# Third FFN layer in (row, feature) form, with the h2 rows stationary, and TensorE's slot order turned

## The chip, the cores and the metric

The kernel runs on one core of a Trainium2 chip. The time is the device time of one execution in microseconds; the time before is 2948.12 us, the median of 3 runs (2947.69 to 2948.82). The profile is one further execution, of 2946.45 us.

## The reference, cut to what matters

The input is x (16 batches, 1024 nodes, 256 features). A graph attention block comes first, then a mixture of 8 experts (E = 8), each a three-layer FFN applied to every row. All experts run on all rows; a gate w, one vector of 8 weights for each of the 1024 nodes, sums them:

```
x = x + attention(layernorm(x), adj)                       # per batch 1024 x 1024
x = x + ffn(layernorm(x))
ffn:  w = softmax(mean over batch of x @ Wr + br)          # 1024 x 8
      h = relu(bn(x @ W1[e] + b1[e]))                      # per expert e
      h = relu(bn(h @ W2[e] + b2[e]))
      y = h @ Wo[e] + bo[e]
      out = sum over e of y * w[:, e]
```

All products are made from split operands: an fp32 value is a "hi" part in fp32r and a "lo" rest in fp32r, and one product is the three matmuls hi*hi, hi*lo and lo*hi.

## The kernel before, in words

`attention_block` (lines 145 to 792) fills roughly the first quarter of the time, `ffn_block` (lines 795 to 1195) the rest. The change is in `ffn_block` alone.

A tile is 512 rows (CT = 4 groups of 128) of one batch; a batch has CH = 2 tiles, and there are 16 batches, so 32 tiles. A step is one expert on one tile: 8 steps a tile, US = 16 steps a batch, 256 in all. Each engine runs `slot(b, u, last)` for u = 0 to 15 in a hardware loop over b of 15 iterations (B - 1), and then the 16 slots once more, written out. Slot u works ahead by different distances: layer 1 of step u + 3, layer 2 of step u + 2, layer 3 of step u + 1. So the pipeline of a step runs over several slots:

- TensorE, `layer` (L944): 12 matmuls for a layer, each 128 x 128 stationary (a block of weights, hi or lo) by 128 x 512 moving (the activations in (feature, row) form, 512 rows). It writes z1_ps, z2_ps or y_ps, two PSUM banks each. `split_matmul` (L50) issues the three matmuls of a product at L52, L53 and L54.
- ScalarE: `bn_relu` (L1048) of layer 1, the hi part of h1 (L1065), `bn_relu` of layer 2.
- VectorE: the lo part of h1 (L1127), the product of h2 with the gate (L1140), the hi part of h2 (L1144), the lo part of h2 (L1146).

Layer 3 sums all eight experts of a tile into y_ps, in (feature, row) form, since the gate is already in h2. At the end of a tile (u % 8 == 7) ScalarE copies y_ps to yT_sb (L1055), TensorE turns it with 8 transposes into turn_ps (`transpose_y`, L935 to 942), and VectorE adds the residual rows from x1_sb (L1153, `out_ready`). SyncE then stores the tile and loads the next one into the same buffer (L869 to 875). `transpose_x` (L925) turns the normalised rows of the next tile in slot u % 8 == 4, into the same PSUM tile turn_ps.

The order on TensorE in a slot is: layer 1 of u + 3, transposes if any, layer 2 of u + 2, layer 3 of u + 1. The order is written out by hand and each engine keeps it. Where a layer starts, TensorE waits for the lo part of its input; for the first expert of a tile layer 3 waits also for `yT_ready`, since y_ps is opened anew.

The gate table, transposed, lay in yT_sb at the start (`wT_sb`), before the first tile used it.

Of the kernel before, what the change touches and what calls it, by code (L numbers as in the profile page):

```python
# [23 lines left out]
ALU = mybir.AluOpType  # L24
# [3 lines left out]
P = 128  # L28
# [766 lines left out]
def ffn_block(nc, B, Wo, x1_dram, w_dram, out, ident, minus_half, node_table, w12_hi, w12_lo,  # L795
# [11 lines left out]
    with ctx:  # L807
        def sb(name, shape, dt=FP32):
            return ctx.enter_context(nc.sbuf_tensor(name, shape, dt))
# [4 lines left out]
        def sem(name):  # L814
# [15 lines left out]
        yT_sb = sb("yT_sb", [P, KB, BANK])  # L830

        wT_sb = yT_sb[0:E, :, :].rearrange("e c n -> e (c n)")
# [12 lines left out]
            step_done yT_ready out_psum out_ready  # L845
# [19 lines left out]
        def _(sp):  # L865
# [17 lines left out]
            sp.dma_start(w_dram.rearrange("e c n -> e (c n)"), wT_sb).then_inc(w_stored, DMA)  # L883
# [40 lines left out]
        def _(pe):  # L924
            def transpose_x(n):  # L925

                pe.wait_ge(norm.xn_ready, n)
                wait(pe, S["out_ready"], n - 2)
# [5 lines left out]

            def transpose_y(n):  # L935

                pe.wait_ge(S["yT_ready"], n)
                for s in range(CT):
                    for d in range(KB):
                        at = (s % 2) * D + d * P  # L940
                        last = pe.transpose(turn_ps[:, s // 2, at:at + P], yT_sb[:, d, s * P:(s + 1) * P], ident[:, :])  # L941
                last.then_inc(S["out_psum"], 1)

            def layer(acc, w_hi, w_lo, x_hi, x_lo, first, last):  # L944

                for m in range(KB):
                    for k in range(KB):
                        at = slice(k * D + m * P, k * D + (m + 1) * P)
                        done = split_matmul(pe, acc[:, m, :], w_hi[:, at], w_lo[:, at], x_hi[:, k, :], x_lo[:, k, :],
                                            first and k == 0, last and k == KB - 1)  # L950
                return done
# [17 lines left out]
            def slot(b, u, last):  # L969
                ok, c, e, n = step_at(b, u, 3, last)  # L970
# [13 lines left out]
                if u >= 0 and u % E == E - 1:  # L984
                    transpose_y(b * CH + (u // E + 1))
# [6 lines left out]
                ok, c, e, n = step_at(b, u, 1, last)  # L992
                if ok:
                    pe.wait_ge(S["h2_lo_ready"], n)
                    if u == -1:
                        pe.wait_ge(S["table_ready"], 1)
                        pe.wait_ge(S["wo_lo_ready"], 2)
                        pe.wait_ge(S["wo_lo_pool_ready"], 2)
                    if e == 0:
                        wait(pe, S["yT_ready"], b * CH + (u + 1) // E)  # L1000
                    layer(y_ps, wo_hi[:, e, :], wo_lo[:, e, :], h2_hi[n_par(u + 1)], h2_lo[n_par(u + 1)],
                          e == 0, e == E - 1).then_inc(S["step_done"], 1)
# [16 lines left out]
            for u in range(1 - LOOK, 0):  # L1019
                slot(0, u, B == 1)  # L1020
# [202 lines left out]
```

## Time and profile before

| what | value |
|---|---|
| median of 3 runs | 2948.12 us (2947.69 to 2948.82) |
| the profiled execution | 2946.45 us, span 2944.7 us |
| TensorE busy | 2884.2 us, 98% of the span |
| VectorE busy | 1931.2 us, 66% |
| ScalarE busy | 1697.9 us, 58% |
| GpSimd busy | 730.2 us, 25% |
| one loop iteration of the FFN part | 16 steps, 15 iterations and one written out |

The span is the time from the first instruction to the last; the execution's own time has 1.75 us more around it. Starts of matmuls, rather than their durations, tell what TensorE costs: the matmuls are pipelined, one is some 0.39 us long and the next starts after some 0.23 us.

### The profile page before, as it was taken

The numbers are of one execution on the slowest core, as the hardware profiler recorded it, in microseconds if no ns is written. First come the engines' busy times: TensorE is split into PE (matmuls) and PEld (weight loads), VectorE is DVE, ScalarE is ACT, GpSimd is POOL, SyncE is SP. The second block draws the span as 40 slices with busy tenths as digits, with TensorE's granted clock in tenths as the row PEclk, the third lists the DMA queues.
The fourth block names the chain that finished last, engine by engine and source line by source line (L and its number), as shares of the span: only waits on it lengthen the run. The fifth ranks groups of instructions, "written<-read, shape, count | busy, mean of one in ns | idle before, by whom it ended". The sixth has DMA issues, their size and how long they took to land.

```text
span 2944.7 us, 42543 instructions
## 1 busy us (share of the span) xinstructions
PE 2884.2 (98%) x14806; PEld 2423.9 (82%) x14806; DVE 1931.2 (66%) x2843; ACT 1697.9 (58%) x2620; POOL 730.2 (25%) x894
## 2 busy tenths in 40 slices
PE   7999999998999999999999999999999999999998
PEld 7989898998888888888888888888888888888887
DVE  7999999996555555655556565556555565655554
ACT  7889888987444545444444445454544444454544
POOL 5888888887100000000000000000000000000000
PEclk9999999999999999999999999999999999999999
DMA  4444444443100000000000000000000000000000
GB/s 153 150 155 155 150 156 152 156 141 111 57 15 14 21 21 14 14 14 14 14 14 14 14 14 14 14 14 14 23 20 14 14 14 14 14 14 14 14 15 15
DMA packets 86037, 145.60 MB, mean 49 GB/s; under 512 B 7744, under 2 KB 63464, under 8 KB 86000
## 3 DMA queue, kind: packets, MB, share of 16 engines
q1 hardware_dynamic: 86000, 145.13, 14.7%
q8 instruction: 20, 0.33, 0.0%
q14 instruction: 17, 0.14, 0.0%
HBM read 111.52 MB, written 33.59 MB: 49 GB/s over the span
## 4 chain that ended last, share of the span: by engine, by line
PE 75%; DVE 0%; ACT 0%; issue 0%
PE z_ps L54 16%; PE z_ps L52 16%; PE z_ps L53 16%; PE y_ps L54 8%; PE y_ps L53 8%; PE y_ps L52 8%; PE turn_ps L931 1%; PE turn_ps L941 1%; PE y_ps L1016 0%; PE turn_ps L965 0%; PE y_ps L965 0%; PE z_ps L1009 0%; PE y_ps L1009 0%; ACT h L1048 0%; DVE h L1140 0%; DVE h_lo L1146 0%
## 5 line engine op out<-in xcount | busy, mean ns | idle before, releaser
L1048 ACT ACTIVATE h<-z_ps,bn_shift,bn_scale 128x512 f32<-128x512 f32 x1024 | 741.8, 775 | 1077.5 <-PE z_ps L54 1075.9
L1127 DVE TENSOR_TENSOR h_lo<-h,h_hi 128x1024 fp32r<-128x1024 f32 x256 | 321.6, 1256 | 762.5 <-ACT h_hi L1065 762.5
L86 POOL TENSOR_TENSOR ffn_vareps<-ffn_mv,ln_eps 128x4 f32<-128x4 f32 x32 | 6.4, 201 | 1880.0 <-DVE ffn_mv L80 1880.0
L52 PE MATMUL z_ps<-h_hi,w_hi 128*128 128x512 f32 x1024 | 410.3, 401 | 0.0
L54 PE MATMUL y_ps<-h_hi,wo_lo 128*128 128x512 f32 x1024 | 406.8, 397 | 0.0
L1140 DVE TENSOR_TENSOR h<-h,w_bc 128x1024 f32<-128x1024 f32 x256 | 313.8, 1226 | 140.9 <-ACT h L1048 137.0
L54 PE MATMUL z_ps<-h_hi,w_lo 128*128 128x512 f32 x1024 | 405.8, 396 | 0.0
L52 PE MATMUL z_ps<-xT_hi,w_hi 128*128 128x512 f32 x1024 | 405.2, 396 | 0.0
L53 PE MATMUL z_ps<-xT_lo,w_hi 128*128 128x512 f32 x1024 | 405.1, 396 | 0.0
L54 PE MATMUL z_ps<-xT_hi,w_lo 128*128 128x512 f32 x1024 | 405.0, 396 | 0.0
L53 PE MATMUL z_ps<-h_lo,w_hi 128*128 128x512 f32 x1024 | 405.0, 395 | 0.0
L53 PE MATMUL y_ps<-h_lo,wo_hi 128*128 128x512 f32 x1024 | 404.7, 395 | 0.0
L52 PE MATMUL y_ps<-h_hi,wo_hi 128*128 128x512 f32 x1024 | 402.3, 393 | 2.0 <-DVE h_lo L1146 2.0
L1146 DVE TENSOR_TENSOR h_lo<-h,h_hi 128x1024 fp32r<-128x1024 f32 x256 | 313.8, 1226 | 8.7
L52 PE MATMUL attn_ps<-wh_hi,pT_hi 128*128 128x256 f32 x1024 | 306.1, 299 | 0.0
L53 PE MATMUL attn_ps<-wh_lo,pT_hi 128*128 128x256 f32 x1024 | 289.2, 282 | 0.0
L54 PE MATMUL attn_ps<-wh_hi,pT_lo 128*128 128x256 f32 x1024 | 289.1, 282 | 0.0
L1065 ACT ACTIVATE h_hi<-h 128x1024 fp32r<-128x1024 f32 x256 | 271.3, 1060 | 9.3
L53 PEld LDWEIGHTS y_ps<-h_lo,wo_hi 128*128 128x128 f32 x1024 | 192.4, 188 | 49.0
L52 PEld LDWEIGHTS y_ps<-h_hi,wo_hi 128*128 128x128 f32 x1024 | 192.3, 188 | 48.5 <-DVE h_lo L1146 2.4
L52 PEld LDWEIGHTS z_ps<-xT_hi,w_hi 128*128 128x128 f32 x1024 | 192.6, 188 | 47.7
L54 PEld LDWEIGHTS z_ps<-xT_hi,w_lo 128*128 128x128 f32 x1024 | 192.5, 188 | 46.8
(128 smaller groups left out, 4876.6 us busy)
## 6 DMA issues: line engine op xcount, KB each, us to landing
adj_sb<-in_adj SPq DMA_DIRECT2D x128, 512.0 KB, 3.4
x_sb<-in_x SPq DMA_DIRECT2D x64, 256.0 KB, 2.8
x_scratch<-x_sb SPq DMA_DIRECT2D x128, 128.0 KB, 1.8
ffn_x<-x_scratch SPq DMA_DIRECT2D x32, 512.0 KB, 3.3
out<-ffn_x SPq DMA_DIRECT2D x32, 512.0 KB, 2.9
w_stage<-in_L_ffn_W SPq DMA_DIRECT2D x16, 256.0 KB, 4.0
w_bc<-w_scratch SPq DMA_DIRECT2D x8, 512.0 KB, 7.3
w_bc<-in_L_ffn_Wo SPq DMA_DIRECT2D x4, 512.0 KB, 5.9
```

The costliest lines, as they stand in the source:

```text
L52: pe.matmul(out, w_hi, x_hi, start=first, stop=False)
L53: pe.matmul(out, w_hi, x_lo, start=False, stop=False)
L54: return pe.matmul(out, w_lo, x_hi, start=False, stop=last)
L86: pool.tensor_tensor(self.vareps[:, :], self.mv[:, :, 1], self.ln_eps[:, :], ALU.add) \
L931: last = pe.transpose(turn_ps[:, d, s * P:(s + 1) * P], norm.xn[:, s, d * P:(d + 1) * P], ident[:, :])
L941: last = pe.transpose(turn_ps[:, s // 2, at:at + P], yT_sb[:, d, s * P:(s + 1) * P], ident[:, :])
L1048: return act.activation(dst[:, m, :], src[:, m, :], ACT.Relu, bias=bn_shift[layer][:, col], scale=bn_scale[layer][:, col])
L1065: act.activation(h1_hi[n_par(u + 3)][:, :, :], h1[:, :, :], ACT.Copy).then_inc(S["h1_hi_ready"], 1)
L1127: dve.tensor_tensor(h1_lo[i][:, :, :], h1[:, :, :], bits(h1_hi[i][:, :, :]), ALU.subtract) \
L1140: dve.tensor_tensor(h2[:, :, :], h2[:, :, :], w_bc[:, c, e, :].unsqueeze(1).to_broadcast([P, KB, BANK]), ALU.mult).then_inc(S["gated_ready ...
L1146: dve.tensor_tensor(h2_lo[i][:, :, :], h2[:, :, :], bits(h2_hi[i][:, :, :]), ALU.subtract) \
```

## The change

Layer 3 is computed with the operands swapped: the stationary operand is a 128 x 128 block of h2 (128 features by 128 rows), the moving one 256 columns of Wo, and the result is 128 rows by 256 features, the form in which the output is stored. One product of three matmuls is needed for each of 4 row groups and 2 halves of the contraction: 24 matmuls of 256 columns in place of 12 of 512. y_ps then holds rows, VectorE adds the residual straight from y_ps, and ScalarE's copy, the transposes and the tile yT_sb go. On TensorE layer 3 of step u now stands at the beginning of slot u; before, it was layer 3 of step u + 1 at the end of slot u. VectorE's addition moves from slot 7 of a tile, behind the work on h2 of slot 7, to slot 6, behind the work on h2 of that slot. Instead of `yT_ready`, TensorE waits for `out_ready` at the end of slot 7 of a tile. `transpose_x` waits for `xT_lo_ready` of the tile before in place of `out_ready`.

```diff
-        yT_sb = sb("yT_sb", [P, KB, BANK])
-        wT_sb = yT_sb[0:E, :, :].rearrange("e c n -> e (c n)")
+        wT_sb = sb("wT_sb", [E, TB * P])
...
             def transpose_x(n):
                 pe.wait_ge(norm.xn_ready, n)
-                wait(pe, S["out_ready"], n - 2)
+                wait(pe, S["xT_lo_ready"], n - 1)
...
-            def transpose_y(n):
-                pe.wait_ge(S["yT_ready"], n)
-                for s in range(CT):
-                    for d in range(KB):
-                        at = (s % 2) * D + d * P
-                        last = pe.transpose(turn_ps[:, s // 2, at:at + P], yT_sb[:, d, s * P:(s + 1) * P], ident[:, :])
-                last.then_inc(S["out_psum"], 1)
...
+            def layer_rows(e, x_hi, x_lo):
+                for s in range(CT):
+                    rows, acc = slice(s * P, (s + 1) * P), y_ps[:, s // 2, (s % 2) * D:(s % 2 + 1) * D]
+                    for k in range(KB):
+                        cols = slice(k * D, (k + 1) * D)
+                        opens = e == 0 and k == 0 and s % 2 == 0
+                        pe.matmul(acc, x_hi[:, k, rows], wo_hi[:, e, cols], start=opens, stop=False,
+                                  skip_group_check=True)
+                        pe.matmul(acc, x_hi[:, k, rows], wo_lo[:, e, cols], start=False, stop=False,
+                                  skip_group_check=True)
+                        done = pe.matmul(acc, x_lo[:, k, rows], wo_hi[:, e, cols], start=False,
+                                         stop=e == E - 1 and k == KB - 1, skip_group_check=True)
+                return done
...
             def slot(b, u, last):            # TensorE
+                if u >= 0:
+                    pe.wait_ge(S["h2_lo_ready"], b * US + (u + 1))
+                    layer_rows(u % E, h2_hi[n_par(u)], h2_lo[n_par(u)]).then_inc(S["step_done"], 1)
...
-                if u >= 0 and u % E == E - 1:
-                    transpose_y(b * CH + (u // E + 1))
...
-                ok, c, e, n = step_at(b, u, 1, last)
-                if ok:
-                    pe.wait_ge(S["h2_lo_ready"], n)
-                    if u == -1:
-                        pe.wait_ge(S["table_ready"], 1)
-                        pe.wait_ge(S["wo_lo_ready"], 2)
-                        pe.wait_ge(S["wo_lo_pool_ready"], 2)
-                    if e == 0:
-                        wait(pe, S["yT_ready"], b * CH + (u + 1) // E)
-                    layer(y_ps, wo_hi[:, e, :], wo_lo[:, e, :], h2_hi[n_par(u + 1)], h2_lo[n_par(u + 1)],
-                          e == 0, e == E - 1).then_inc(S["step_done"], 1)
+                if u >= 0 and u % E == E - 1 and not (last and u == US - 1):
+                    pe.wait_ge(S["out_ready"], b * CH + (u // E + 1))
...
                 slot(0, u, B == 1)
+            pe.wait_ge(S["table_ready"], 1)
+            pe.wait_ge(S["wo_lo_ready"], 2)
+            pe.wait_ge(S["wo_lo_pool_ready"], 2)
...
             def slot(b, u, last):            # ScalarE
-                if u >= 0 and u % E == E - 1:
-                    act.wait_ge(S["step_done"], b * US + (u + 1))
-                    act.activation(yT_sb[:, :, :], y_ps[:, :, :], ACT.Copy).then_inc(S["yT_ready"], 1)
...
-                if u >= 0 and u % E == E - 1:
+                if u >= 0 and u % E == E - 2:
                     t = u // E
-                    dve.wait_ge(S["out_psum"], b * CH + (t + 1))
+                    dve.wait_ge(S["step_done"], b * US + (u + 2))
                     dve.wait_ge(S["residual_ready"], b * CH + (t + 1))
                     rows = x1_sb[t][:, :, :].rearrange("p s d -> p (s d)")
-                    dve.tensor_tensor(rows, turn_ps[:, :, :].rearrange("p k c -> p (k c)"), rows, ALU.add) \
+                    dve.tensor_tensor(rows, y_ps[:, :, :].rearrange("p k c -> p (k c)"), rows, ALU.add) \
                         .then_inc(S["out_ready"], 1)
```

## Rows read from the trace of the kernel before

**Rows 1.** The page: busy times; VectorE's tenths and the granted clock in 40 slices.

```profile
PE 2884.2 (98%) x14806; PEld 2423.9 (82%) x14806; DVE 1931.2 (66%) x2843; ACT 1697.9 (58%) x2620; POOL 730.2 (25%) x894
...
DVE  7999999996555555655556565556555565655554
...
PEclk9999999999999999999999999999999999999999
```

**Rows 2.** Windows of 137.8 us, each an FFN iteration: busy (count), clock, DMA, GB/s.

```profile
744.70:882.50 137.80, 137.80 (x607) 111.38 (x606) 78.32 (x90) 67.13 (x84) 9.94 (x7) 1.00 0.05 16
1433.90:1571.70 137.80, 137.80 (x609) 111.43 (x608) 80.68 (x92) 67.16 (x85) 9.18 (x6) 1.00 0.04 15
```

**Rows 3.** Timeline of SyncE: the same store in two iterations that follow each other.

```profile
1441.12 0.38 SPq L871 DMA_DIRECT2D out<-ffn_x  x1
1578.96 0.39 SPq L871 DMA_DIRECT2D out<-ffn_x  x1
```

**Rows 4.** Timeline of TensorE around transpose_y and layer 3: start, length.

```profile
1499.88 0.40 PE L54 MATMUL z_ps<-xT_hi,w_lo 128*128 128x512 f32 x1
1500.11 1.04 PE L941 MATMUL turn_ps<-ident,yT_sb 128*128 128x128 f32 x8
1500.90 0.48 PE L52 MATMUL z_ps<-h_hi,w_hi 128*128 128x512 f32 x1
1501.22 0.39 PE L53 MATMUL z_ps<-h_lo,w_hi 128*128 128x512 f32 x1
...
1503.77 0.39 PE L52 MATMUL y_ps<-h_hi,wo_hi 128*128 128x512 f32 x1
...
1506.58 0.39 PE L52 MATMUL z_ps<-xT_hi,w_hi 128*128 128x512 f32 x1
```

**Rows 5.** Timeline of TensorE in the attention part, 256 columns, 24 in a row.

```profile
385.74 0.28 PE L53 MATMUL attn_ps<-wh_lo,pT_hi 128*128 128x256 f32 x1
385.86 0.28 PE L54 MATMUL attn_ps<-wh_hi,pT_lo 128*128 128x256 f32 x1
...
388.49 0.60 PE L462 MATMUL head_ps<-ident,x_sb 128*128 128x128 f32 x4
```

**Rows 6.** TensorE's waits over the whole span: us in total, times, longest.

```profile
PE y_ps L52 <- DVE h_lo L1146: 2.0, 1, 2.0
PE turn_ps L941 <- ACT yT_sb L1055: 1.1, 1, 1.1
```

**Rows 7.** Timeline of VectorE at a tile's end.

```profile
1429.33 1.23 DVE L1146 TENSOR_TENSOR h_lo<-h,h_hi 128x1024 fp32r<-128x1024 f32 x1
1433.97 1.23 DVE L1127 TENSOR_TENSOR h_lo<-h,h_hi 128x1024 fp32r<-128x1024 f32 x1 [3.41 <-ACT h_hi L1065]
1439.74 1.22 DVE L1153 TENSOR_TENSOR ffn_x<-turn_ps,ffn_x 128x1024 f32<-128x1024 f32 x1
```

**Rows 8.** Timelines of ScalarE and TensorE at the same place.

```profile
1428.59 1.03 ACT L1055 ACTIVATE yT_sb<-y_ps 128x1024 f32<-128x1024 f32 x1 [1.35 <-PE y_ps L54]
...
1434.85 0.39 PE L52 MATMUL y_ps<-h_hi,wo_hi 128*128 128x512 f32 x1
```

**Rows 9.** The chain of waits at the end of the span: start, us, what.

```profile
2937.56 0.25 PE y_ps L54
2937.81 0.02 issue
2937.83 1.03 ACT yT_sb L1055
2938.86 0.04 issue
2938.91 1.11 PE turn_ps L941 x8
2940.01 0.02 issue
2940.04 1.23 DVE ffn_x L1153
```

**Rows 10.** Groups by form: attention weight loads, then a matmul of 258 fp32 columns.

```profile
L53 PEld LDWEIGHTS attn_ps<-wh_lo,pT_hi 128*128 128x128 f32 x1024 | 195.7, 191 | 1.7
L476 PE MATMUL head_ps<-wx,hT 128*128 128x258 f32 x480 | 119.0, 390 | 0.0
```

**Rows 11.** DMA queues: window 744:883; window 883:2812; a small load's us to landing.

```profile
q8 instruction: 5, 0.08, 0.2%
...
q1 hardware_dynamic: 18816, 29.36, 4.5%
...
a_sb<-in_L_gnn_a SPq DMA_DIRECT2D x2, 1.0 KB, 2.4
```

More of the change, by code:

```diff
@@ L844, in ffn_block @@
             z1_ready h1_ready h1_hi_ready h1_lo_ready z2_ready relu2_ready gated_ready h2_hi_ready h2_lo_ready
-            step_done yT_ready out_psum out_ready
+            step_done out_ready
             featT_psum featT_ready logits_psum logits_ready top_ready centred_ready exp_ready total_ready
@@ L882, in _ @@
             sp.wait_ge(S["wT_ready"], 1)
-            sp.dma_start(w_dram.rearrange("e c n -> e (c n)"), wT_sb).then_inc(w_stored, DMA)
+            sp.dma_start(w_dram.rearrange("e c n -> e (c n)"), wT_sb[:, :]).then_inc(w_stored, DMA)
             sp.wait_ge(w_stored, DMA)
@@ L1035, in copy_gate @@
                 act.wait_ge(S["wT_psum"], 1)
-                act.activation(wT_sb, y_ps[0:E, :, :].rearrange("e k c -> e (k c)"), ACT.Copy) \
+                act.activation(wT_sb[:, :], y_ps[0:E, :, :].rearrange("e k c -> e (k c)"), ACT.Copy) \
                     .then_inc(S["wT_ready"], 1)
```

## The prediction

> **What bounds the kernel now.** The page comes first: TensorE is busy 98% of the span at full granted clock, while VectorE and ScalarE stand at 66% and 58% [rows 1]. Then the windows of one FFN iteration: TensorE is busy for all of the 137.80 us, in the first iteration and in a later one, with VectorE at 81 and ScalarE at 67 [rows 2]. Last the waits: in the whole FFN part TensorE waits once for h2 (2.0 us) and once for yT_sb (1.1 us), both at the very end [rows 6]. So the FFN part lasts as long as TensorE's queue takes from start to start, and an edit counts by what it does to that sum. Two stores of the same tile slot lie 1578.96 - 1441.12 = 137.84 us apart [rows 3]: that is the iteration.
>
> I price TensorE's pieces by starts. Eight transposes: without them the first matmul of layer 2 would start at 1500.11 and the second 0.233 later; the second starts at 1501.22, so the eight cost 1501.22 - 1500.11 - 0.233 = 0.87 us [rows 4]. An iteration has 48 layers and 4 such bundles (two of x, two of y): (137.84 - 4 x 0.87) / 48 = 2.799 us a layer, 0.2333 us a matmul of 512 columns; layer 3 in the timeline, 1503.77 to 1506.58, agrees [rows 3, 4].
>
> **The change, part by part.**
>
> 1. The transposes of y go: 31 times 0.87 us on the bounding engine, -27.0 us. The 32nd belongs to the end of the span, below.
>
> 2. Layer 3 becomes 24 matmuls of 256 columns. The columns streamed are the same, 6144; what is new is 12 more matmuls and 12 more weight loads a step. The FFN part has no such matmul, but the attention part has: 128 x 128 stationary, 256 moving columns, fp32r, the order hi, hi, lo, summed into half a bank. From 385.74 to the transpose behind the block at 388.49 are 23 starts: 2.75 / 23 = 0.1196 us; another pair gives 0.12 [rows 5]. That is 2.9 ns more than half of 0.2333. 24 x 0.1196 to 0.1200 is 2.87 to 2.88 us against 2.80, so +0.073 us a step (I take the longer baseline's value, 0.1197 rounded), and for 256 steps +18.7 us. Weight loads are no bound of their own at that pace: in those same attention rows each lasts 191 ns while they follow each other every 0.12 us [rows 5, 10]. Ends: below, the pace of the transposes, 8 in 0.87 us or 0.109 us a load and matmul (24 make 2.62 us, -46 us in all) [rows 4]; above, a matmul of 258 columns in plain fp32: each is 390 ns long against 0.28 us for the attention matmuls [rows 5, 10], and if the starts spread in that proportion, 0.167 us each, it would be 256 x (4.01 - 2.80) = +310 us. Its number format is another, so I give that end no weight; the value of the same form stands. The decisive point is thin: 1.7 ns a matmul more than 0.1197 eats the whole gain.
>
> 3. The turned order. Listed one behind the other, layers were 1(u+3), 2(u+2), 3(u+1), 1(u+4), ...; they are 3(u), 1(u+3), 2(u+2), 3(u+1), ...: the same sequence, with the loop's seam moved from before layer 1 to before layer 3. Distances between a layer and its consumer stay, apart from the 0.87 us that go and the 0.07 that come. Price nothing. Each iteration is busy throughout with the branch in it [rows 2], so the seam costs nothing today, with queued matmuls covering it.
>
> 4. The new wait. Layer 3 of a tile's first expert now needs `out_ready`. VectorE makes it in its slot 6: behind the lo part of h2 (start 1429.33, 1.23 long, ends 1430.56). The last layer 3 of the old tile was done at 1428.59, when ScalarE began its copy, so the addition (1.22 us, the same size and also out of PSUM) runs 1430.6 to 1431.8 [rows 7, 8]. TensorE's layer 3 stood at 1434.85 with the transposes in front; without them it stands at 1433.98 [rows 4, 8]. The slack is 2.1 us. Price nothing. Queued behind the wait on TensorE's queue are the branch (second tile of a batch) and layer 3 itself; VectorE's next instruction, L1127, came at 1433.97 and waited 3.41 us for ScalarE, so the earlier addition delays nothing there [rows 7]. It leaves VectorE's slot 7, where it stood alone at 1439.74.
>
> 5. ScalarE loses 32 copies of 1.03 us, SyncE's store and reload start some 9 us sooner, `transpose_x` has a wait long satisfied. All beside TensorE; nothing. The own wT_sb and the three waits before slot 0 are work of the prologue in the same order; nothing (ends: 1 us either way).
>
> 6. The end of the span. From the last layer 3 the chain went copy, transposes, addition: ScalarE began at 2937.83, VectorE at 2940.04 [rows 9]. Now VectorE follows at once: -2.2 us. The 0.07 us of the last layer is in the 18.7.
>
> Sum: -27.0 + 18.7 - 2.2 = -10.5 us. The profiled execution took 2946.45 us, so 2935.9; the median of the runs is 1.67 us above it, so 2937.6, written as 2938 (-0.3%).
>
> 7. More instructions. An iteration has 609 matmuls and 608 weight loads [rows 2] and would have 192 - 16 = 176 more of each: some 1,570 in place of 1,217. In the first iteration the instruction queue brought 5 packets, 0.08 MB, which is 16 KB a packet and some 66 bytes an instruction; in the next 14 iterations it brought none (the only queue with traffic from 883 to 2812 us is q1) [rows 11]. So a body of about 5 blocks stays on the chip; the new one, by the same bytes, is 6.3 blocks, and no row shows a body of that size. If it doesn't stay, the branch back needs a fetch. The first pass, whose blocks come while it runs, has no idle time [rows 2, 11], so blocks in sequence are hidden; only the target of the branch could be late. The ends for that are nothing (queued matmuls cover it) and 2.4 us, the landing time of a small load [rows 11], 14 times. I take nothing, being nearer to the row of a body that is held.
>
> The Trainium skill, Runtime: NRT & Kernel Launch, section Instruction fetch mechanics, says that a taken branch whose target is outside a window of two pages must wait for a fetch. The trace disagrees: a loop of 5 blocks ran 14 times with no instruction packet. The same section gives TensorE 128 KiB, eight blocks of 16 KiB, in contradiction to its two; by that figure (an estimate) the new body, 6.3 blocks laid over 7 or 8 block borders with one fetched ahead, lies right at the edge. By the one rule every pass pays today already, and the change brings nothing new; by the other the case turns on the body's place.
>
> **The rivals.**
>
> A. Refetch at the seam (slower). The longer body isn't held, and each of 14 branches exposes up to 2.4 us: up to 2937.6 + 34 = 2971. Moreover the branch now stands right behind the wait of part 4, so fewer matmuls are queued ahead of it. It decides from 10.5 / 14 = 0.75 us a branch. For it: nothing of that length was seen to be held; against: 5 blocks are held with ease and a first pass hides all its fetches. Half exposed, 2954. Chance 12%.
>
> B. Matmuls of 256 columns cost more beside h2 than in attention (same, or a little slower). There the stationary blocks were written long before; here VectorE and ScalarE write their pair tiles beside them. 2 to 3 ns more each: 2950 to 2956. For it: only the smallness of the margin; against: in the attention part, the first quarter of the slices, VectorE was busier than here [rows 1]. Chance 10%.
>
> C. The pair pace of 0.109 us holds (faster): -46 - 29.2 from 2948.12, that is 2873. Against: the 256-column rows themselves. Chance 4%.
>
> D. The wait on `out_ready` takes the place of the transposes: it would have to come over 2.1 us late; every microsecond beyond costs 31 us (one late: 2969). For it: it sits behind one more VectorE instruction than the old wait did. Chance 4%.
>
> Forecast: 70%.
>
> **How the numbers follow.** A measurement of this kernel tells 0.2% (5.9 us) from no change. Forecast and C are faster, except the forecast's edge above 2942.2, for which I take 5 points: 0.69. Same: those 5, half of B, and the part of A with little exposed: 0.14. Slower: the rest, 0.17. The likeliest case alone reaches from 2935 (0.1193 us a matmul and a free seam) to 2942. The range for 8 in 10 leaves out C below and the fully exposed halves of A and D above: 2931 to 2957.
>
> **What would show it.** Right: an iteration of 137.84 - 1.74 + 16 x 0.073 = 137.3 us between stores; 256-column matmuls of y_ps starting every 0.12 us; no row of waits for L1153 on TensorE; VectorE's addition right behind L1146 in slot 6; chain's end going from y_ps straight to the addition. Wrong: instruction packets between the first and the last iteration with idle TensorE after a branch (A); starts 0.122 us apart or more (B) or near 0.11 (C); TensorE idle on VectorE's addition (D).

## The result and the profile after

| what | before | after |
|---|---|---|
| median of 4 runs each | 2947.93 us (2947.69 to 2948.82) | 2926.29 us (2924.61 to 2926.85) |
| ratio, 95% interval | | 0.9925 [0.9908, 0.9942] |
| the profiled execution | 2946.45 us, span 2944.7 us | 2924.61 us, span 2922.8 us |

The change made the kernel faster by about 22 us, or 0.75%. The forecast was 10 us and its range ended at 2931, so it had the sign and half of the size.

The page of after has TensorE at 98% again, with 2816 more matmuls and 2816 more weight loads than in [rows 1]; ScalarE has lost its 32 copies and 34 us. The last line is the instruction queue of the whole run: 23 packets.

```profile
PE 2862.9 (98%) x17622; PEld 2553.2 (87%) x17622; DVE 1931.4 (66%) x2843; ACT 1663.6 (57%) x2588; POOL 730.0 (25%) x894
...
q8 instruction: 23, 0.38, 0.1%
```

One iteration in the windows of after (busy us and count of TensorE, weight loads, VectorE, ScalarE, GpSimd; then clock, DMA share, GB/s). TensorE is busy for all of it, as in [rows 2]:

```profile
1290.10:1426.60 136.50, 136.50 (x786) 119.49 (x785) 80.62 (x92) 65.05 (x83) 9.16 (x6) 1.00 0.05 15
```

The timeline of SyncE, the same store in two iterations (start, length), answers to [rows 3]: 1563.03 - 1426.48 = 136.55 us, against 137.84 before and 137.3 forecast.

```profile
1426.48 0.38 SPq L869 DMA_DIRECT2D out<-ffn_x  x1
...
1563.03 0.39 SPq L869 DMA_DIRECT2D out<-ffn_x  x1
```

The timeline of TensorE in after, the first matmul of each layer of one step and of the next layer 3 (start, length):

```profile
1445.50 0.28 PE L949 MATMUL y_ps<-wo_hi,h_hi 128*128 128x256 f32 x1
...
1448.35 0.39 PE L52 MATMUL z_ps<-xT_hi,w_hi 128*128 128x512 f32 x1
...
1451.13 0.40 PE L52 MATMUL z_ps<-h_hi,w_hi 128*128 128x512 f32 x1
...
1453.93 0.28 PE L949 MATMUL y_ps<-wo_hi,h_hi 128*128 128x256 f32 x1
```

Here is the difference. Layer 3 takes 1448.35 - 1445.50 = 2.85 us, layer 1 2.78, layer 2 2.80. Before, all three took 2.80. As medians over some 255 steps of the trace, start to start, in us:

| kernel | layer 3 | layer 1 | layer 2 | a step against before |
|---|---|---|---|---|
| before | 2.800 | 2.800 | 2.800 | |
| after | 2.849 | 2.782 | 2.796 | +0.027 |

256 steps by 0.027 are +6.9 us, where the forecast had +18.7. That difference, 11.8 us, is the profiled execution's distance from the forecast made against it (2935.9 - 2924.61 = 11.3) within half a microsecond. So close an agreement is partly luck: in the profiles of this document the attention part, whose work is the same in all of them, ends up to 2 us earlier or later.

The waits of TensorE in after that belong to the FFN part (us in all, times, longest). Each comes once, the first ahead of the loop and the second in the pass written out behind it, and none names the addition:

```profile
PE turn_ps L929 <- PEq L168: 5.2, 1, 5.2
PE y_ps L949 <- DVE h_lo L1141: 1.9, 1, 1.9
```

The timeline of VectorE at a tile's end, answering to [rows 7]: the addition (L1148) stands right behind the lo part of h2. Below it is the first matmul of the next tile's layer 3, from TensorE's timeline.

```profile
1423.96 1.23 DVE L1141 TENSOR_TENSOR h_lo<-h,h_hi 128x1024 fp32r<-128x1024 f32 x1
1425.10 1.22 DVE L1148 TENSOR_TENSOR ffn_x<-y_ps,ffn_x 128x1024 f32<-128x1024 f32 x1
```

```profile
1428.65 0.28 PE L949 MATMUL y_ps<-wo_hi,h_hi 128*128 128x256 f32 x1
```

The addition ends at 1426.32, so it is 2.33 us early here, behind a branch; at the tile ends inside the loop body it is 2.40 us early.

The end of the chain, answering to [rows 9]: from the last matmul of layer 3 straight to the addition.

```profile
2918.05 0.13 PE y_ps L953
2918.18 0.02 issue
2918.20 1.23 DVE ffn_x L1148
```

### The profile page after: what moved, and what is told of

The parts are those of the page before. It is cut to its first block, busy times and chain, and to the rows that moved or that the text cites. A ratio compares the mean times of both kernels' runs of the same rounds, so it can differ in the third digit from the quotient of the medians.

```text
span 2922.8 us, 48112 instructions
## 1 busy us (share of the span) xinstructions
PE 2862.9 (98%) x17622; PEld 2553.2 (87%) x17622; DVE 1931.4 (66%) x2843; ACT 1663.6 (57%) x2588; POOL 730.0 (25%) x894
## 4 chain that ended last, share of the span: by engine, by line
PE 75%; DVE 0%; ACT 0%; ACTq 0%; issue 0%
PE z_ps L54 16%; PE z_ps L53 16%; PE z_ps L52 16%; PE y_ps L949 8%; PE y_ps L951 8%; PE y_ps L953 8%; PE turn_ps L929 1%; PE y_ps L1012 0%; PE turn_ps L969 0%; PE y_ps L969 0%; PE z_ps L1005 0%; PE y_ps L1005 0%; DVE h L1135 0%; DVE h_lo L1141 0%; DVE ffn_x L1148 0%; PE y_ps L960 0%
## 5 line engine op out<-in xcount | busy, mean ns | idle before, releaser
L949 PE MATMUL y_ps<-wo_hi,h_hi 128*128 128x256 f32 x2048 | 576.3, 281 | 1.9 <-DVE h_lo L1141 1.9
L951 PE MATMUL y_ps<-wo_lo,h_hi 128*128 128x256 f32 x2048 | 575.7, 281 | 0.0
L953 PE MATMUL y_ps<-wo_hi,h_lo 128*128 128x256 f32 x2048 | 574.6, 281 | 0.0
L949 PEld LDWEIGHTS y_ps<-wo_hi,h_hi 128*128 128x128 f32 x2048 | 386.8, 189 | 13.4 <-DVE h_lo L1141 2.1
L951 PEld LDWEIGHTS y_ps<-wo_lo,h_hi 128*128 128x128 f32 x2048 | 385.7, 188 | 12.1
L953 PEld LDWEIGHTS y_ps<-wo_hi,h_lo 128*128 128x128 f32 x2048 | 386.8, 189 | 0.0
L54 PEld LDWEIGHTS z_ps<-h_hi,w_lo 128*128 128x128 f32 x1024 | 193.9, 189 | 46.1
```

The source lines that it names most:

```text
L54: return pe.matmul(out, w_lo, x_hi, start=False, stop=last)
L949: pe.matmul(acc, x_hi[:, k, rows], wo_hi[:, e, cols], start=opens, stop=False, skip_group_check=True)
L951: pe.matmul(acc, x_hi[:, k, rows], wo_lo[:, e, cols], start=False, stop=False, skip_group_check=True)
L953: done = pe.matmul(acc, x_lo[:, k, rows], wo_hi[:, e, cols], start=False, stop=e == E - 1 and k == KB - 1, skip_group_check=True)
```

## The experiments

All times are medians of several runs, the ratio is to the kernel before on the same chip; its medians there lay between 2947.36 and 2948.56 us. "After" and "before" name the kernel that was edited. Layer lengths are medians as in the table above.

### Where the 12 us are: width, order of roles, transposes

**After with layer 3 wide again**, y added without having been turned, so that y's form in the output is not the reference's:

```diff
-                    layer_rows(u % E, h2_hi[n_par(u)], h2_lo[n_par(u)]).then_inc(S["step_done"], 1)
+                    e = u % E
+                    layer(y_ps, wo_hi[:, e, :], wo_lo[:, e, :], h2_hi[n_par(u)], h2_lo[n_par(u)],
+                          e == 0, e == E - 1).then_inc(S["step_done"], 1)
```

> The changed kernel with layer 3 put back to 12 matmuls of 512 columns with the weights stationary, in the new slot order and without the transposes of y, so y is added unturned (that part of the result is left in the wrong form). Theory W: all three layers at 2.800 us, and 31 x 0.87 + 2.2 us less than before: 2919. Theory O (turned order or missing transposes quicken the other layers): layer 1 at 2.78 us here too, 2913 to 2915.

Measured: 2918.45 us (2917.61 to 2920.23), ratio 0.9903 [0.9886, 0.9919]. The timeline of TensorE in this kernel, first matmul of each layer:

```profile
1444.36 0.39 PE L52 MATMUL y_ps<-h_hi,wo_hi 128*128 128x512 f32 x1
...
1447.16 0.39 PE L52 MATMUL z_ps<-xT_hi,w_hi 128*128 128x512 f32 x1
...
1449.96 0.39 PE L52 MATMUL z_ps<-h_hi,w_hi 128*128 128x512 f32 x1
...
1452.76 0.39 PE L52 MATMUL y_ps<-h_hi,wo_hi 128*128 128x512 f32 x1
```

Each layer is 2.80 us, in the turned order too. So the order alone does nothing to the pace, and the kernel without the transposes of y and with the short tail is 28.9 us below before (2947.36), where steps 1 and 6 of the prediction say 27.0 + 2.2 = 29.2. What the narrow form costs is then 2926.29 - 2918.45 = 7.8 us, across two sessions, not 18.7.

**Before with layer 3 in 24 matmuls of 256 columns**, weights still stationary:

```diff
+            def layer_narrow(acc, w_hi, w_lo, x_hi, x_lo, first, last):
+                for m in range(KB):
+                    for s in range(2):
+                        rows = slice(s * D, (s + 1) * D)
+                        for k in range(KB):
+                            at = slice(k * D + m * P, k * D + (m + 1) * P)
+                            pe.matmul(acc[:, m, rows], w_hi[:, at], x_hi[:, k, rows], ...)
+                            pe.matmul(acc[:, m, rows], w_hi[:, at], x_lo[:, k, rows], ...)
+                            done = pe.matmul(acc[:, m, rows], w_lo[:, at], x_hi[:, k, rows], ...)
...
-                    layer(y_ps, wo_hi[:, e, :], ...)
+                    layer_narrow(y_ps, wo_hi[:, e, :], ...)
```

> The kernel before with one edit: each 512-column matmul of layer 3 is split into two of 256 columns; weights stay stationary, transposes and order stay. Theory W (the width does it: 256-column matmuls cost 118.7 ns in layer 3, and the 512-column layers behind them run at some 231.8 to 233 ns a matmul instead of 233.3): layer 3 2.85 us, layer 1 2.78, layer 2 2.80, so +0.03 us a step and +7 us: 2955. Theory S (the swap of the operands does it): layer 3 at the attention part's pace, 2.87 to 2.88 us, layers 1 and 2 at 2.80, +18 to +20 us: 2966 to 2968.

Measured: 2987.56 us (2984.32 to 2990.49), ratio 1.0133 [1.0116, 1.0150]. Neither theory had this. Its layers are 2.868, 2.782 and 2.797 us: layers 1 and 2, whose code is that of before, are as short as in after. So, with the tiles where they lie in these kernels, it is the narrow layer beside them that shortens them, and neither the stationary h2 nor the order does it. Layer 3 itself is 0.019 us longer than in after, at the same width; with the swap of the operands and the turned order both undone here, this run does not tell which of them it is. The paces give 256 x 0.047 = +12 us; the other 28 lie elsewhere. Its timeline around a branch, then TensorE's waits, then the line of the instruction queue (packets, MB, share):

```profile
1451.83 0.28 PE L965 MATMUL y_ps<-h_hi,wo_lo 128*128 128x256 f32 x1
1453.86 0.49 PE L52 MATMUL z_ps<-xT_hi,w_hi 128*128 128x512 f32 x1 [1.76 <-issue]
```

```profile
PE z_ps L52 <- issue: 21.7, 14, 1.9
```

```profile
q8 instruction: 149, 2.44, 0.3%
```

TensorE stands still at each of the 14 branches back, waiting for nothing but an instruction, and the queue brought 149 packets of 16 KB instead of after's 23. This is rival A, in another kernel: its loop body has 1,641 recorded TensorE instructions, before's 1,257, after's 1,608. The waits are 21.7 of the 28 us. Most of the rest is the clock: behind the wait in three of the 14 passes the granted clock fell to the lower of its two levels, 1.2 GHz, and matmuls of 512 columns started every 0.43 us in place of 0.23. The window of the first of the three, as a row like that of [rows 2]:

```profile
1031.00:1036.00 5.00, 4.65 (x13) 3.72 (x14) 1.56 (x2) 0.07 (x1) 0.00 (x0) 0.66 0.33 111
```

**Before with only the twelfth matmul of each layer 3 in two halves:**

```diff
+    parts = (slice(0, D), slice(D, BANK)) if i == which else (slice(0, BANK),)   # which = 11
```

> The kernel before with only the last matmul of each layer 3 split into two of 256 columns (13 matmuls instead of 12). Theory W, in the form that one narrow matmul ahead of a layer is enough to set its pace: layer 1 falls to 2.78 us, layer 3 rises by 0.005 us, so 2948 - 4 = 2944. If the pace needs a whole narrow layer, or isn't due to the width: layer 1 stays at 2.80, and the time is 2948 to 2950.

Measured: 2950.81 us (2949.06 to 2951.37), ratio 1.0010 [1.0000, 1.0019]; layers 2.806, 2.799 to 2.801, 2.802. One narrow pair does not shorten the neighbours.

**After with the three products of layer 3 in the order of `split_matmul`** (lo by hi second):

```diff
-                        pe.matmul(acc, x_hi[:, k, rows], wo_lo[:, e, cols], ...)
-                        done = pe.matmul(acc, x_lo[:, k, rows], wo_hi[:, e, cols], ...)
+                        pe.matmul(acc, x_lo[:, k, rows], wo_hi[:, e, cols], ...)
+                        done = pe.matmul(acc, x_hi[:, k, rows], wo_lo[:, e, cols], ...)
```

> The changed kernel with the three matmuls of a product in layer 3 in another order: x_hi by wo_hi, x_lo by wo_hi, x_hi by wo_lo (before: x_hi by wo_hi, x_hi by wo_lo, x_lo by wo_hi), so the stationary block changes at each matmul and the moving one is repeated. Theory P (the pace of a run of matmuls is a pattern set by their addresses and order): layer 3 leaves 2.849 us by up to 0.03 either way, up to +-8 us. Rival (the cost is that of a 256-column matmul, whatever the order): 2.849 us and 2926.

Measured: 2926.43 us (2924.39 to 2927.11), ratio 0.9924 [0.9908, 0.9941]; layers 2.849, 2.782, 2.796, all unchanged.

### The longer loop body (rival A)

The instruction queue brings one 16 KB packet for some 256 TensorE instructions: after's program has 5,984 recorded ones, each counted once however often its loop runs, and 23 packets. Counted in such blocks, after's body of 1,608 touches 7 and ends some 11 instructions short of the next border, since the first packet behind the loop came 11 recorded instructions behind the last branch. The idea to be tested: a body that touches 7 blocks is held, one that touches 8 is brought anew in every pass. Four kernels, all edited from after.

**48 instructions ahead of the loop**, the body unchanged:

```diff
-                for it in range(TB):
+                for it in list(range(TB)) * 4:
                     last = pe.transpose(y_ps[0:E, it // CT, ...)
```

> The changed kernel with the gate's 8 transposes issued four times: 48 instructions more ahead of the loop (2.6 us of work once), the body itself as it was. Theory F by block borders: the body now begins 29 instructions before the same border and ends beyond the last one, so it touches eight blocks and is fetched anew: 2953 to 2963. Rival L (length alone): 2929, no packets in the later passes.

Measured: 2970.32 us (2969.05 to 2971.74), ratio 1.0074 [1.0057, 1.0091]. TensorE's waits, and the instruction queue of the page:

```profile
PE y_ps L949 <- issue: 24.2, 14, 2.2
...
PE y_ps L953 <- issue: 6.0, 9, 1.2
```

```profile
q8 instruction: 149, 2.44, 0.3%
```

Not one instruction of the loop was touched, it was only moved by 48, and the kernel lost 44 us and became slower than before; 1 us of them lies ahead of the loop, where the added transposes are. The 126 packets more than after's are 9 for each of 14 passes: the 8 blocks that the body touches, and one more. This is more than the 2953 to 2963 expected, for two reasons. A second stall comes inside the body (L953). And in six of the 14 passes the granted clock fell to 1.2 GHz right behind the wait at the branch, here from 1442.5 us on:

```profile
1441.88 0.38 PE L949 MATMUL y_ps<-wo_hi,h_hi 128*128 128x256 f32 x1 [1.95 <-issue]
...
1444.13 0.41 PE L949 MATMUL y_ps<-wo_hi,h_hi 128*128 128x256 f32 x1
1444.35 0.41 PE L951 MATMUL y_ps<-wo_lo,h_hi 128*128 128x256 f32 x1
```

Starts are 0.22 us apart there, in place of 0.12. The two kinds of waits are 30 us, and the clock explains most of the rest.

**16 waits more in the body** (satisfied since long ago), which takes its end over the border by some 4 or 5 (1,623 instructions are recorded, where the expectation counted 1,624):

```diff
                 if u >= 0:
+                    pe.wait_ge(S["w_ready"], 1)
                     pe.wait_ge(S["h2_lo_ready"], b * US + (u + 1))
```

> The changed kernel with one more wait a slot on TensorE, on a semaphore long satisfied: 16 instructions more in the loop body, 1,624 recorded in place of 1,608, no work. Theory F (the body of the changed kernel ends some 11 instructions short of a 16 KB block border, and a body that touches an eighth block is fetched anew in each pass): over 90 instruction packets and 1.5 to 2.1 us of idle time at each of 14 branches, 2926 + 25 to 35 = 2951 to 2961. Rival L (only a length between 1,608 and 1,641 counts, wherever the body lies) leaves it open. Rival N (the idle time of the kernel with narrow matmuls in the old roles had another cause): 2926.

Measured: 2937.96 us (2929.85 to 2942.36), ratio 0.9962 [0.9950, 0.9975]. Waits and queue:

```profile
PE y_ps L949 <- issue: 7.7, 4, 2.9
```

```profile
q8 instruction: 59, 0.97, 0.1%
```

Only some passes fetch: the 36 packets more than after's are 9 for each of four passes, and those four have the waits. The runs scatter over 12 us. The +11.7 us are less than half of the 25 to 35 expected; right at the border the case is not all or nothing.

**Both: 16 waits in the body and 96 instructions ahead** (`* 7` in place of `* 4`), so that by the count the longer body starts just behind a border and touches 7 blocks:

> The 16 waits in the body, and the gate's transposes issued seven times, 96 instructions ahead of the loop (5.2 us once). Theory F by block borders: the body of 1,624 now begins behind a border and touches seven blocks: no packets, 2926 + 5 = 2931. Rival L with a limit below 1,624, or rival in which the packets of the 16-wait kernel came from the waits: 2956 to 2966.

Measured: 2930.30 us (2930.02 to 2931.68), ratio 0.9941 [0.9924, 0.9958]. No wait for an instruction is left in the FFN part, and the queue:

```profile
q8 instruction: 24, 0.39, 0.1%
```

A longer body at a better place is held, and its 4 us above after lie ahead of the loop, where the added transposes are: the way from the attention part to the loop's first branch back is 4.0 us longer than in after. That settles it: the place of the body against the blocks decides, not its length alone.

**Two batches in a pass**, 3,214 recorded instructions in the body, 7 passes:

```diff
-                with pe.Fori(0, B - 1) as b:
-                    for u in range(US):
-                        slot(b, u, False)
+            with pe.Fori(0, B // 2 - 1) as p:
+                for half in range(2):
+                    for u in range(US):
+                        slot(p * 2 + half, u, False)
```

> The changed kernel with the FFN loop over pairs of batches: a body of 32 slots, twice as many instructions (some 3,200, 0.2 MB), 7 passes. Theory F (a body over a certain length isn't held and is fetched anew in each pass): some 12 instruction packets of 16 KB a pass on the instruction queue, and at each of the 7 branches TensorE may be late by up to 2.4 us: 2926 to 2943. Rival (any length is held, or a fetch at the branch is hidden by queued matmuls): 2926, with no idle time of TensorE; the packets tell the two apart.

Measured: 2941.90 us (2935.34 to 2946.90), ratio 0.9983 [0.9973, 0.9992]: +15.6 us. TensorE's waits, then the queue in the window 900 to 2700 us, where before had none [rows 11]:

```profile
PE y_ps L949 <- issue: 9.0, 6, 1.9
```

```profile
q8 instruction: 97, 1.59, 0.4%
```

The profiled execution was the fastest of ten, 2935.34 us, 10.7 above after's profiled one, and the waits at its six branches back are 9.0 of these. So blocks in sequence are for the most part hidden, the target of a branch is not. Where the other executions lost up to 11 us more, no trace shows.

### The new wait (step 4, rival D)

**Two operations of the addition's size ahead of it**, 2.35 us on VectorE:

```diff
+                    for extra in range(2):
+                        dve.tensor_tensor(spare[:, extra, :], y_ps[:, :, :].rearrange("p k c -> p (k c)"), rows, ALU.add)
                     dve.tensor_tensor(rows, y_ps[:, :, :].rearrange("p k c -> p (k c)"), rows, ALU.add) \
```

> The changed kernel with two further VectorE operations of the addition's size ahead of it at each tile's end, so out_ready comes 2.4 us later. Theory of slack (out_ready has 2.1 us to spare before layer 3 of the next tile): TensorE waits some 0.3 us and a restart at each of 31 tile ends: 2926 + 10 to 25 = 2936 to 2951. Rival Z (less slack, the wait already bounds or nearly does): + 2 us or more a tile, 2990. Rival Y (more slack than worked out): 2926.

Measured: 2937.81 us (2935.88 to 2938.96), ratio 0.9966 [0.9953, 0.9978]: 11.5 us. The waits of TensorE show the part that falls behind the branch:

```profile
PE y_ps L950 <- issue: 4.0, 14, 0.3
```

By VectorE's timeline the addition starts 2.26 us later for them. At the tile ends inside the body this costs nothing that can be read (layer 2 is as long as elsewhere), which fits the 2.40 us that were free there. At those behind a branch layer 3 starts 0.45 us late, though 2.33 us were free, and a pass takes 137.12 us in place of 136.55, 8 us in 14 passes. So the slack of 2.1 us that the prediction read is right inside the body, on the safe side; behind a branch some 1.8 of it can be used. The rest of the 11.5 us lies ahead of the loop and behind it, where executions differ anyway.

### What sets the pace: where the operands lie

**32 bytes of padding ahead of the activation tiles** (x1, xT, h1, h2), so that they move against the weights:

```diff
+        pad = sb("pad", [P, 8])
         x1_sb = [x1_first, sb("ffn_x11", [P, CT, D])]
```

> The changed kernel with 32 bytes of unused SBUF ahead of the FFN's activation tiles, so that xT, h1 and h2 lie 32 bytes further against the weights. Theory A (the pace of a layer hangs on where its operands lie to each other): the layers leave 2.849, 2.782 and 2.796 us by 0.01 or more. Rival (the widths in the stream set it): the same to 0.002 us, 2926.

Measured: 2942.96 us (2940.31 to 2943.83), ratio 0.9981 [0.9971, 0.9992], that is 16.7 us more than after. The timeline of TensorE, firsts of the layers:

```profile
1443.21 0.28 PE L950 MATMUL y_ps<-wo_hi,h_hi 128*128 128x256 f32 x1
...
1446.09 0.40 PE L52 MATMUL z_ps<-xT_hi,w_hi 128*128 128x512 f32 x1
...
1448.88 0.40 PE L52 MATMUL z_ps<-h_hi,w_hi 128*128 128x512 f32 x1
...
1451.69 0.28 PE L950 MATMUL y_ps<-wo_hi,h_hi 128*128 128x256 f32 x1
```

Medians 2.878, 2.797, 2.811: a step is 0.059 us longer than after's, 15 us in 256. The same instructions in the same order, with 32 bytes between their tiles, take back three quarters of the gain. Layer 1 is back at 2.797 us, with the narrow layer still ahead of it: the shortening of the neighbours hangs on where the tiles lie, too.

**Everything moved by 32 or by 64 bytes**, all distances kept (a pad of 8 or 16 fp32 ahead of the weights):

```diff
+        pad_all = keep("pad_all", [P, 8])          # and [P, 16]
         w12_hi = keep("w12_hi", [P, 2, E, KB * D], FP32R)
```

> The same with 32 bytes, so that every distance is kept and every tile changes sides of a 64-byte border. Theory D: 2.849, 2.782 and 2.796 us, 2926. Theory G, or a rule by 64-byte borders for single operands: layers 1 and 2, whose operands both leave their borders, rise above 2.80.

> The changed kernel with 64 bytes of unused SBUF ahead of the W1/W2 tiles: every weight and activation tile of the FFN moves by 64 bytes, none against another. Theory D (only the distances between operands count): the layers stay at 2.849, 2.782 and 2.796 us, 2926. Theory G (the place itself counts, in a pattern longer than 64 bytes): some layer moves by 0.01 us or more.

Measured: by 32 bytes 2925.60 us (2925.21 to 2925.99), ratio 0.9925 [0.9896, 0.9954]; by 64 bytes 2925.78 (2925.66 to 2925.91), ratio 0.9926 [0.9897, 0.9954]. The timeline of the kernel moved by 32:

```profile
1446.84 0.28 PE L950 MATMUL y_ps<-wo_hi,h_hi 128*128 128x256 f32 x1
...
1449.69 0.39 PE L52 MATMUL z_ps<-xT_hi,w_hi 128*128 128x512 f32 x1
...
1452.47 0.40 PE L52 MATMUL z_ps<-h_hi,w_hi 128*128 128x512 f32 x1
```

Layers 2.849, 2.782, 2.796 in both. Moving the tiles as a whole by 32 or 64 bytes does nothing; moving the activations alone does.

**Wo moved by 32 bytes and the activations by 64**, tried first as a rule of borders, in three kernels: after, before, and the one with Wo's halves side by side (below).

```diff
+        pad_wo = sb("pad_wo", [P, 8])
         wo_hi, wo_lo = sb("wo_hi", [P, E, KB * D], FP32R), sb("wo_lo", [P, E, KB * D], FP32R)
...
+        pad_x = sb("pad_x", [P, 8])
         x1_sb = [x1_first, sb("ffn_x11", [P, CT, D])]
```

> The changed kernel with 32 bytes of unused SBUF ahead of the weight tiles and 32 more behind them: wo_hi and wo_lo now start on a multiple of 64 bytes (before: 32 bytes off one), xT, h1 and h2 stay on one. Theory A (an operand that starts 32 bytes off a multiple of 64 costs the matmul about 1 ns; the attention part's tiles, 0.1197, and layer 3 with the padded h2, 0.1199, have both operands off, layer 3 of the changed kernel only the moving one, 0.1187): with both on, layer 3 falls to 2.82 to 2.835 us, 3 to 7 us less: 2919 to 2923; layers 1 and 2 as before. Rival (what counts is the distance between the two operands, which the 32-byte pad of the other run also changed): layer 3 rises to 2.87, 2932.

> The kernel before with the same two pads: wo on a multiple of 64 bytes. Theory A: layer 3, whose stationary operand is wo there, drops below 2.800 us, by up to 0.02, 2943 to 2948. Rival (in a stream of 512-column matmuls alone, 2.800 us is the floor, wherever the operands lie): 2948 and 2.800 in all three layers.

> The kernel with x_hi against both halves of Wo in one matmul, with the same two pads. Theory A: layer 3 2.77 us in place of 2.789, 2906 to 2909. Rival of the distance: 2914 to 2918.

| edited from | median us (range) | ratio | layer 3, 1, 2 | against its base |
|---|---|---|---|---|
| after | 2929.01 (2928.30 to 2929.51) | 0.9936 [0.9920, 0.9953] | 2.843 or 2.849, 2.792, 2.800 | +2.7 |
| before | 2943.89 (2943.51 to 2945.16) | 0.9987 [0.9977, 0.9996] | 2.783 or 2.798, 2.795 or 2.800, 2.795 | -4.6 |
| halves side by side | 2921.24 (2920.73 to 2922.39) | 0.9911 [0.9895, 0.9928] | 2.806, 2.794, 2.800 | +9.7 |

The rule of borders fell: one gained, two lost. Its rival, that the distance between a layer's own two operands sets its pace, fell with it: in the first row h2 lies 32 bytes further from Wo than in after, just as with the 32 bytes of padding above, and layer 3 takes 2.843 or 2.849 us here against 2.878 there.

Two values in a field are two groups of about the same number. In the kernel before, layer 3 takes 2.783 and 2.798 us in turn from step to step, as its two buffers of h2 alternate. So a wide layer among wide ones can run at 2.783 us as well, without any narrow matmul: what looked like an effect of the neighbours' width is not theirs alone. Since this kernel gained 4.6 us from padding alone, before too stood on a placement that was not its best.

**The same pad ahead of the attention part's pT tiles**, beside those of the third row:

```diff
+        pad_pt = sb("pad_pt", [P, 8])
         pT_hi = [sb(f"pT_hi{i}", [P, TB, P], FP32R) for i in range(2)]
```

> The kernel of the run above with 32 bytes ahead of the attention part's pT and wh tiles too, so that they start on a multiple of 64 bytes. Theory A: its 3,072 matmuls of 256 columns fall from 0.1197 to about 0.1175 us, where TensorE bounds that part: up to 6 us less than the run above, 2901 to 2906. Rival (TensorE waits for the others there, or the distance counts): no change, 2907 to 2909.

Measured: 2922.02 us (2921.81 to 2922.29), ratio 0.9913 [0.9896, 0.9929]; matmuls of the attention block start every 119.8 ns on average, against 119.6 without the pad. No effect there; but the tiles of both its operands lie behind the pad and moved together, so this run tells nothing of their distance.

### A version that beats both

**Wo's hi and lo halves side by side**, so that a hi block of h2 meets both in one matmul of 512 columns, into a bank of its own; the two halves of the bank are added by VectorE, which adds twice. 16 matmuls a step in place of 24. y_ps takes four banks, and the turning of x goes to z1_ps at the start of slot 5.

```diff
-        wo_hi, wo_lo = sb("wo_hi", [P, E, KB * D], FP32R), sb("wo_lo", [P, E, KB * D], FP32R)
+        wo = sb("wo", [P, E * KB, 2, D], FP32R)
...
+                        pe.matmul(y_ps[:, s, :], x_hi[:, k, rows], wo[:, e * KB + k, :, :].rearrange("p h d -> p (h d)"), ...)
+                        done = pe.matmul(y_ps[:, s, 0:D], x_lo[:, k, rows], wo[:, e * KB + k, 0, :], ...)
...
+                    dve.tensor_tensor(rows, y_ps[:, :, D:], rows, ALU.add).then_inc(S["half_ready"], 1)
+                    dve.wait_ge(S["half_ready"], b * CH + (t + 1))
+                    dve.tensor_tensor(rows, y_ps[:, :, 0:D], rows, ALU.add) \
```

> The changed kernel with fewer, wider matmuls in layer 3: Wo's hi and lo parts lie side by side, so an x_hi block meets both in one matmul of 512 columns (sums in the two halves of a bank, y_ps four banks), and x_lo meets wo_hi in one of 256: 16 matmuls a step in place of 24. The transposes of x go into z1_ps at the start of slot 5, since the banks of turn_ps are gone; VectorE adds twice at a tile's end. Theory W (the cost is a sum over matmuls, 118.7 ns for 256 columns and 232 for 512): layer 3 is 8 x (0.232 + 0.119) = 2.81 us in place of 2.849, -10 us: 2916. Rival H (the three layers fall back to 2.80 with so few narrow ones, as in the kernel with 512 columns alone): 2.81, 2.80 and 2.80: 2921. Rival Q (the second addition or the transposes ahead of layer 3 open a new wait of about 0.5 to 1 us a tile): 2930 to 2950.

Measured: 2911.57 us (2910.70 to 2913.24), ratio 0.9876 [0.9860, 0.9893]. Its timeline of TensorE, firsts of the layers:

```profile
1441.87 0.40 PE L948 MATMUL y_ps<-wo,h_hi 128*128 128x512 f32 x1
...
1444.65 0.39 PE L52 MATMUL z_ps<-xT_hi,w_hi 128*128 128x512 f32 x1
...
1447.44 0.39 PE L52 MATMUL z_ps<-h_hi,w_hi 128*128 128x512 f32 x1
...
1450.23 0.40 PE L948 MATMUL y_ps<-wo,h_hi 128*128 128x512 f32 x1
```

Layers 2.789, 2.782, 2.796. The neighbours are as short as in after with eight narrow matmuls in the step, and layer 3 itself no longer pays for being narrow: 2.81 us and a kernel of 2916 were expected, and it went 4.4 us below. TensorE has no wait for the two additions. The body is 1,353 recorded instructions, shorter than after's. It is 14.7 us below after, of which the layers' paces give 15.4.

## Why the prediction was wrong, and where it was right

**Step 1, the transposes, and step 6, the tail: right.** The wide kernel without them is 28.9 us faster, against 29.2; the run holds the two terms together, not each by itself. The chain's end goes the way that was said.

**Step 2, layer 3 in 24 matmuls: the mechanism right, the size off.** This is the term that failed: "+0.073 us a step ... for 256 steps +18.7 us". The narrow layer took 2.849 us, 118.7 ns a matmul, not 119.7; that is +0.049 us a step, 12.5 us. The price came from the attention part [rows 5], where the operands lie elsewhere. The experiments show that layer 3's pace depends on the placement (2.849 or 2.878 us by 32 bytes), and that it is 2.868 us with the old roles and order; that the attention part's price is higher for this reason is likely, not shown. A small slip in the sum adds to it: 2.75 / 23 is 0.1196, not 0.1197, which makes the term about +18. The text called it thin, 1.7 ns a matmul more would have eaten the gain, and weighed as rivals only prices above the row (B) or far below it (C). Below the row its likeliest case reached just to 0.1193 us and 2935; 1 ns is 6 us.

**Step 3, the turned order: right for the order, but "Price nothing" also covered the untouched layers.** Those were assumed to stay at 2.799 us. They went to 2.782 and 2.796, 0.022 us a step, 5.6 us. The narrow layer in the kernel before, with its old roles and order, does the same to them; the wide layer in the turned order does not. The two errors, 6.2 + 5.6 = 11.8 us, account for the 11.3 us that the forecast was short.

**Step 4, the new wait: right**; the slack is 2.3 to 2.4 us by the rows, where 2.1 were read, and rival D did not come. **Step 5: not contradicted.** The sum leaves a remainder of 0.5 us, but executions of one kernel differ by 2 us, so a term of that size would not be seen.

**Step 7, the longer body: right in the result, by 11 instructions.** Rival A is a real mechanism. That its time was met (up to 2971 forecast; 2970.32 with 48 instructions put ahead) is luck: it reckoned with at most 2.4 us a branch on top of 2937.6, and the runs show about 3 us a pass, with the second stall and the fallen clock in it, on top of 2926.3. What the argument lacked was the body's place: 6.3 blocks were compared with the 5 that were held, and the answer depended on where the first block's border fell. No row before the runs told how many blocks are held, so the forecast was right here by luck; with that number, counting the TensorE instructions ahead of the loop decides the case. The Trainium skill, Runtime: NRT & Kernel Launch, section Instruction fetch mechanics, gives TensorE 128 KiB, refilled in blocks of 16 KiB, and, for a branch, a window of two pages. The runs disagree with the second, as [rows 11] did. They agree with the first, which makes eight blocks, if one of the eight is the block fetched ahead; the ninth packet of each pass that was fetched anew fits that, but it is an argument, not shown.

**B** was wrong in sign, **C** far off: the pair pace of the transposes, 109 ns, is not the 118.7 ns of 256 columns.

**Open.** Why one placement of the tiles is better than another, which distances count (those of a layer's own operands are not enough), and whether the narrow layer shortens the wide ones behind it by the same cause. So the sizes of the two failed terms are measured, and their cause stays open; no row names a resource.

## What to carry to other kernels

Where TensorE is the bound and fully busy, a price per matmul taken from another place of the kernel was good to about 1% here, and with 6,144 such matmuls 1% was 7 us: allow it to go either way, and allow the neighbours' pace to change too. Before a hardware loop grows, count its blocks of 256 instructions from where they really begin; 48 instructions ahead of the loop cost 44 us. And where a product is split in hi and lo and PSUM has the room, the two halves of the moving operand can lie side by side, so that the hi block is loaded once for both.

## What the runs showed of the hardware

- TensorE's instructions come in packets of 16 KB, one for 256. A loop body that touched 7 such blocks was not fetched again in 14 passes (23 or 24 packets in the whole run); one that touched 8 was fetched anew in each (149 packets) and left TensorE idle for 1.2 to 2.2 us at each branch back. Where the eighth block was touched by only some 4 or 5 instructions, four of the passes fetched (59 packets).
- Behind such a wait of 1.7 to 2.2 us the granted clock fell to 1.2 GHz in three of 14 passes in one kernel and in six of 14 in another, and starts went from 0.23 to 0.43 us (512 columns) or from 0.12 to 0.22 us (256 columns).
- Matmuls of split operands with 512 moving columns started every 233.3 ns among their like and every 231.8 ns in layer 1 behind a layer of 24 or of 8 narrow ones; one narrow pair did not do it. It is not the narrow ones alone: with 32 bytes of padding layer 1 was back at 233.1 ns, and with other padding a wide layer among wide ones ran at 231.9 ns in every other step.
- The pace depends on how the tiles lie to each other on chip: 32 bytes between weights and activations made the layers 2.878, 2.797 and 2.811 us in place of 2.849, 2.782 and 2.796, +16.7 us in the kernel; moving all tiles together by 32 or 64 bytes changed nothing (2925.60 and 2925.78 against 2926.29). The distance between a layer's own operands does not settle it: layer 3 took 2.878 us in one kernel and 2.843 or 2.849 in another with the same distance of h2 from Wo.
